# A graph layer on one core: 80 chunks gathered and 63 groups counted, with fp32 one-hots

## The reference

```python
h  = x @ node_w.T
rf = edge_attr_64 @ review_w.T
m  = (h[src] + rf) * edge_weight1
agg = segment_sum(m, dst, num_segments=12500)      # dst is sorted
y = x + agg
out = (y - mean(y)) / sqrt(var(y) + 1e-5)          # over the 64 features
```

## Time and profile before

| what | us |
|---|---|
| median of 3 runs | 4986.41 (4982.99 to 4995.05) |
| the profiled execution: its span, first to last instruction | 4978.1 |
| the profiled execution's own time outside the span | not given; the median lies 8.3 above the span |
| PE busy with matmuls | 2706.6 (54%) |
| DVE busy | 1848.4 (37%) |
| ACT busy | 832.4 (17%) |
| POOL busy | 2097.5 (42%) |
| mean granted TensorE clock | 0.722 of full |

### The profile page before, as it was taken

The page is one execution under the profiler, slowest core; times in us unless marked ns, Lnnn a source line. Parts: engine busy times, 40 slices in busy tenths (PEclk is TensorE's granted clock), DMA queues, the critical chain, the costliest instruction groups (busy, mean ns, idle before and its releaser), DMA issues.

```text
span 4978.1 us, 63532 instructions
## 1 busy us (share of the span) xinstructions
PE 2706.6 (54%) x22003; PEld 2036.4 (41%) x22004; DVE 1848.4 (37%) x7016; ACT 832.4 (17%) x1327; POOL 2097.5 (42%) x2223
## 2 busy tenths in 40 slices
PE   0555555545655545555456555555554556455465
PEld 0343444434443434444344434344443444344345
DVE  3333333423442333333334424333333344333344
ACT  0111111111121111121111211111111112111112
POOL 7343343443334443444433344434444333544432
PEclk9776777767776767777667767677776777667677
DMA  4111121111111111211111211112111112112111
GB/s 98 37 34 37 34 42 38 34 36 38 37 38 38 34 35 38 41 38 34 35 38 35 42 37 35 34 38 42 38 34 35 37 36 42 37 34 43 36 35 38
DMA packets 531458, 192.11 MB, mean 39 GB/s; under 512 B 489893, under 2 KB 495772, under 8 KB 530975
## 3 DMA queue, kind: packets, MB, share of 16 engines
q1 hardware_dynamic: 334128, 80.80, 8.6%
q0 software_dynamic: 70400, 72.23, 6.6%
q10 hardware_dynamic: 126623, 34.94, 3.2%
HBM read 184.60 MB, written 3.20 MB: 38 GB/s over the span
## 4 chain that ended last, share of the span: by engine, by line
PE 43%; another core or an unknown queue 28%; issue 21%; DVE 4%; ACT 2%; DVEq 1%; ACTq 1%; POOLq 0%; POOL 0%
PE x_sums_ps L896 15%; PE count_ps L881 15%; PE window_ps L839 11%; ACT counts L744 2%; DVE scatter L441 1%; DVE hot_lo L497 1%; PE attr_ps L873 1%; ACTq L771 0%; PE turn_ps L858 0%; PE turn_ps L855 0%; DVEq L422 0%; DVEq L425 0%; DVE hot_key L495 0%; PE count_ps L924 0%
## 5 line engine op out<-in xcount | busy, mean ns | idle before, releaser
L366 POOL DMA_INDIRECT rows<-x,src x2200 | 2088.8, 949 | 2791.5 <-DMA src<-src 2146.3
L881 PE MATMUL count_ps<-hot_key,hot_lo 128*128 128x343 bf16 x5550 | 1157.4, 361 | 1294.2 <-ACT counts L744 839.0
L896 PE MATMUL x_sums_ps<-counts,x_tab 128*64 128x126 f32 (+1 forms) x10192 | 865.5, 302 | 790.2 <-issue 775.0
L881 PEld LDWEIGHTS count_ps<-hot_key,hot_lo 128*128 128x128 bf16 x5550 | 570.1, 113 | 1726.5 <-issue 1092.5
L896 PEld LDWEIGHTS x_sums_ps<-counts,x_tab 128*64 128x64 f32 x10192 | 692.5, 154 | 948.4 <-issue 927.3
L744 ACT ACTIVATE counts<-count_ps 128x686 f32<-128x686 f32 x925 | 737.3, 802 | 1784.9 <-remote 1335.6
L495 DVE TENSOR_SCALAR hot_key<-count,cols 128x686 bf16<-128x686 f16 x925 | 377.8, 408 | 1550.8 <-remote 1272.3
L441 DVE TENSOR_SCALAR scatter<-column,dst_left,w 128x128 f32<-128x128 f32 x2200 | 588.3, 347 | 576.2 <-PE window_ps L839 503.0
L497 DVE TENSOR_SCALAR hot_lo<-count,cols 128x128 bf16<-128x128 f16 x2775 | 721.7, 323 | 4.9 <-issue 4.9
L839 PE MATMUL window_ps<-scatter,rows 128*128 128x128 f32 x4400 | 563.1, 289 | 85.2 <-issue 55.4
L839 PEld LDWEIGHTS window_ps<-scatter,rows 128*128 128x128 f32 x4400 | 535.0, 200 | 120.9 <-issue 108.8
(11 more groups left out here) (112 smaller groups left out, 557.5 us busy)
## 6 DMA issues: line engine op xcount, KB each, us to landing
rows<-edge_attr SPq DMA_DIRECT2D x88, 800.0 KB
rows<-x,src POOLq DMA_INDIRECT x2200
g_attr<-edge_attr ACTq DMA_DIRECT2D x51, 576.0 KB
out<-x_tab SPq DMA_DIRECT2D x11, 256.0 KB
counts<-dst SPq DMA_DIRECT2D x1, 1562.5 KB
src<-src SPq DMA_DIRECT2D x88, 12.5 KB, 1.7
dst<-dst SPq DMA_DIRECT2D x88, 12.5 KB
w<-edge_weight SPq DMA_DIRECT2D x88, 12.5 KB
```

Source lines behind the costliest of these rows:

```text
L366: pool.indirect_dma_start(out=rows[:, s, k, 0:F], out_offset=None, in_=x, in_offset=bass.IndirectOffsetOnAxis(ap=src_sb[s][:, k:k + 1].bit ...
L881: last = pe.matmul(count_ps[b][:, a, 0:HALF], hot_lo[h][:, i, :], hot_key[h][:, a * HALF:(a + 1) * HALF], start=(i == 0), stop=(i == 2))
L896: done = pe.matmul(x_sums_ps[half * F:(half + 1) * F, 0:ns], x_tab[:, hi, :], counts[:, hi, 0:ns], start=(hi < 2), stop=(hi >= HI - 2))
```

## The change

Eight chunks less are gathered, and their 200 tiles are counted: 63 groups (0 to 62), the first with 9 tiles. The round becomes ten steps, two of them with two chunks, in a loop of 6 passes, and two last steps of two chunks follow. `hot_key` and `hot_lo` become fp32, `hot_lo` is made once with the whole weight, and the product is two fp32 matmuls. `prepare` and `turn_cols` lose the two cut parts of the weight. `w_both` moves into the space of `counts`, and a store of a block with no whole row of nodes is left out.

```diff
-CHUNKS = 88
-STEPS = (2, 1, 2, 1, 2)
-LAST_STEPS = (2, 2, 2, 2, 2, 2)
+CHUNKS = 80
+STEPS = (1, 1, 1, 1, 2, 1, 1, 1, 1, 2)
+LAST_STEPS = (2, 2)
...
-        KEY, LO, W1, W2, REL, W0 = range(6)
+        KEY, LO, REL, W0 = range(4)
...
-        hot_key = [sb(f"hot_key{b}", [P, HI * SPAN], BF16) for b in range(HOT_BUFS)]
-        hot_lo = [sb(f"hot_lo{b}", [P, 3, P], BF16) for b in range(HOT_BUFS)]
+        hot_key = [sb(f"hot_key{b}", [P, HI * SPAN]) for b in range(HOT_BUFS)]
+        hot_lo = [sb(f"hot_lo{b}", [P, P]) for b in range(HOT_BUFS)]
...
-                    for i, part in enumerate((W0, W1, W2)):
-                        made = dve.tensor_scalar(hot_lo[h][:, i, :], count16[:, 0:P], cols[:, LO, t:t + 1],
-                                                 cols[:, part, t:t + 1], ALU.is_equal, ALU.mult)
+                    made = dve.tensor_scalar(hot_lo[h][:, :], column[:, :], cols[:, LO, t:t + 1],
+                                             cols[:, W0, t:t + 1], ALU.is_equal, ALU.mult)
...
-                    for i in range(3):
-                        for a in range(2):
-                            last = pe.matmul(count_ps[b][:, a, 0:HALF], hot_lo[h][:, i, :],
-                                             hot_key[h][:, a * HALF:(a + 1) * HALF], start=(i == 0), stop=(i == 2))
+                    for a in range(2):
+                        last = pe.matmul(count_ps[b][:, a, 0:HALF], hot_lo[h][:, :],
+                                         hot_key[h][:, a * HALF:(a + 1) * HALF], start=True, stop=True)
```

More of the change, by code:

```diff
@@ L123, in build @@
         g_attr = sb("g_attr", [P, GT, F])
-        hi_lo = sb("hi_lo", [GT, 2, P], I32)
+        src_hi = sb("src_hi", [GT, P], I32)
         tile_first = sb("tile_first", [GT, 1])
-        w_cut = sb("w_cut", [GT, 2, P], BF16)
-        KEY, LO, W1, W2, REL, W0 = range(6)
+        KEY, LO, REL, W0 = range(4)
         packed = sb("packed", [GT, W0, P])
@@ L176, in build @@
         at, g_worst = part(at, 1, [1, 2])
+        at, w_both = part(at, F, [1, 2 * F])
         at, calm = part(at, 1, [4, LATE_CHUNKS])
         assert at <= HI * NS
-        w_both = sb("w_both", [F, 2 * F])
         w_t = sb("w_t", [2 * F, 2 * F])
@@ L334, in _ @@
                     "(a t e) -> a t e", a=1, e=P)).then_inc(g_dst_loaded, 16)
-            sp.dma_start(w_both[:, 0:F], node_w).then_inc(w_loaded, 16)
-            sp.dma_start(w_both[:, F:2 * F], review_w).then_inc(w_loaded, 16)
+            sp.dma_start(w_both[:, 0, 0:F], node_w).then_inc(w_loaded, 16)
+            sp.dma_start(w_both[:, 0, F:2 * F], review_w).then_inc(w_loaded, 16)
             for s in range(SLOTS):
@@ L350, in _ @@
                 whole = min(j, BY_P - h0)
-                sp.dma_start(out[h0 * P:(h0 + whole) * P, :].rearrange("(h l) f -> l h f", l=P),
-                             x_tab[:, h0:h0 + whole, :]).then_inc(stored, 16)
+                if whole:
+                    sp.dma_start(out[h0 * P:(h0 + whole) * P, :].rearrange("(h l) f -> l h f", l=P),
+                                 x_tab[:, h0:h0 + whole, :]).then_inc(stored, 16)
                 if whole < j:
                     sp.dma_start(out[BY_P * P:NODES, :], x_tab[0:NODES - BY_P * P, BY_P, :]).then_inc(stored, 16)
-            sp.wait_ge(stored, 16 * (BLOCKS + (BY_P < HI)))
+            sp.wait_ge(stored, 16 * (sum(h0 < BY_P for h0, _ in blocks) + (BY_P < HI)))
         @block.gpsimd
@@ L466, in prepare @@
                     dve.wait_ge(turned, g)
-                src_i, dst_i, w_i = g_idx[0:nt, 0, :], g_idx[0:nt, 1, :], g_w[0:nt, :]
-                cut, pack, parts = w_cut[0:nt, :, :], packed[0:nt, :, :], hi_lo[0:nt, :, :]
+                src_i, dst_i = g_idx[0:nt, 0, :], g_idx[0:nt, 1, :]
+                pack, hi_i = packed[0:nt, :, :], src_hi[0:nt, :]
                 dve.tensor_reduce(tile_first[0:nt, :], dst_i, AX_X, ALU.min).then_inc(prep_step, 1)
[L470 to L480, removed]
+                dve.tensor_scalar(hi_i, src_i, LO_BITS, None, ALU.arith_shift_right).then_inc(prep_step, 1)
+                dve.wait_ge(prep_step, 4 * g + 2)
+                dve.tensor_scalar(src_i, src_i, P - 1, None, ALU.bitwise_and).then_inc(prep_step, 1)
+                dve.tensor_scalar(pack[:, REL, :], dst_i, tile_first[0:nt, 0:1], None, ALU.subtract
+                                  ).then_inc(prep_step, 1)
+                dve.wait_ge(prep_step, 4 * g + 4)
+                dve.scalar_tensor_tensor(pack[:, KEY, :], hi_i, float(SPAN), pack[:, REL, :],
                                          ALU.mult, ALU.add)
[L482 to L485, removed]
+                dve.tensor_copy(pack[:, LO, :], src_i).then_inc(prepared, 1)
             def make_hot(g, tiles):
@@ L938, in _ @@
             pe.wait_ge(w_loaded, 32)
-            pe.transpose(w_t_ps[:, 0:F], w_both[:, :], ident[0:F, 0:F]).then_inc(w_turned, 1)
+            pe.transpose(w_t_ps[:, 0:F], w_both[:, 0, :], ident[0:F, 0:F]).then_inc(w_turned, 1)
             pe.wait_ge(w_t_ready, 1)
```

## The result

Forecast: 5076 us, slower by 1.8%. Measured: 4831.19 us, median of 4 runs (4823.56 to 4864.78), against 4989.44 (4982.99 to 4995.05) for the kernel before in the same set. The ratio on record, made from all runs, is 0.9699 [0.9665, 0.9733] (the two medians alone give 0.968): faster by 3.0%, outside the range of 4990 to 5225 on the low side. One later kernel, e3_more_records, has a run (4759.51) more than 1.5% above its fastest (4636.36): its ratio leaves that run out, and its trace is of that run. The profiled execution has a span of 4822.8 us, against 4978.1.

What follows compares the result with a forecast made beforehand. Bound: some 60 TensorE instructions pass during a chunk's gathers, about half the span; the rest is TensorE's own speed. 4993 - 24 + 99 = 5068 in the span, 5076 us as median, slower by 1.8%; range 4990 to 5225.

Steps and rivals of the forecast that it cites:

- Bound: Whole kernel: while POOL's gathers fly TensorE passes some 60 instructions, about half the span; the rest is TensorE's own speed.
- Split alone: Fewer gathered chunks and more groups, without fp32: span 4993 us, 15 above 4978.1.
- fp32 at full speed: TensorE's fp32 counting outside the stall: 1.25 us a tile, where bf16 took 0.98 to 1.0.
- rival 3: TensorE counting: fp32 streams one column a cycle, -3.6 us a phase, 4754 us; chance 0.04.
- fp32 counting during a gather: TensorE beside POOL's gathers: 58 instructions at 10 a tile pass 5.8 tiles instead of 4; bounds 4 and 7.3.
- S: Stretch from a gather's start with TensorE counting and `sum_x` in a one-chunk step: mean 67.2 us before, forecast 68.3.
- C: Stretch from a gather's start with TensorE counting in a two-chunk step: mean 54.3 us before, forecast 55.9.
- Phase: A counting phase with split and fp32: 11.6 us left after the stall, 1.6 longer; 62 phases give +99 us.
- Rival 2: Counting during gathers: the stall lets 7.3 of the shorter tiles through, -0.3 us a phase, 4958 us; chance 0.12.
- Rival 1: Counting during gathers: fp32 instructions cost more, only 4 tiles pass, +3.9 us a phase, 5219 us; chance 0.20.
- Rival 4: DVE's longer `hot_key` holds POOL's gathers up, 2 us in each of 62 stretches: +124, 5200 us; chance 0.04.
- -0.5 in S: Shorter DVE one-hots ahead of `scatter` and two transposes less: -0.5 us in each of 48 S, -24 us.

Runs made afterwards that it cites:

- e3_more_records: Kernel after plus one unused one-column fp32 product ahead of each tile's two, with the stall: 4688.53 us, 0.9482 of the kernel before.
- e1: fp32 one-hots alone, without the split (old 88 chunks, 52 groups), against the kernel before, with the stall: 4789.01 us, ratio 0.9736.
- e2: Split alone (80 chunks, 63 groups) with the old three bf16 parts, against the kernel before, with the stall: 4935.32 us, ratio 1.0016.
- i1: Kernel after with eleven one-element POOL fills behind each gather, with the stall: 4028.47 us, 0.8084 of the kernel before.
- j1: Split alone, three bf16 parts, with eleven POOL fills behind each gather, with the stall: 4037.38 us, 0.8068 of the kernel before.
- j2: Split with only two bf16 parts made and multiplied, eleven POOL fills behind each gather, with the stall: 3911.37 us, 0.7831 of the kernel before.
- e5: Split in bf16, TensorE leaving out the third part's products (DVE still makes all three), with the stall: 4659.78 us, 0.9447 of the kernel before.
- f1_after_again: Kernel after, unchanged, run again in a set without the stall: 2903.02 us, 1.0311 of the kernel before.

## Why the prediction was wrong

- **Bound.** Right for this set of runs: for about half of the span TensorE gets through some 60 instructions in 29 us while gathers run. The sentence that this takes 7 us "at full speed" read TensorE's busy time in the stall (7.32 at a clock of 0.56); four tiles at the prediction's own 0.98 are 4 us. Nothing in the sum hangs on it. That the stall isn't in the kernel alone, and that the same program takes 2814 us in another set, no view of one trace could show.
- **Split alone**, +15: right (1.0016). The 2 us in it for group 0 count ten instructions a tile, which is fp32's number and not the split's; that is too small to matter.
- **fp32 at full speed**, 1.25 a tile: right (1.27), and at half clock 4 x 0.57. That rules out rival 3.
- **fp32 counting during a gather**: the step that failed. "58 to 64 instructions, whatever their type and size" gave 58 / 10 = 5.8 tiles. Measured are 97 instructions, 9.7 tiles, in the stretch that stands for 42 of 60, and 70 instructions, 7.0 tiles, in the one that stands for the other 18; 80 or more was the prediction's own sign of being wrong. Two things were wrong. First, I took the beginning of my window for the beginning of the stall: bf16 counting had passed 58 instructions in the first 4 us, fp32 counting needs 8 us for as many, so they lay inside the window. In the 18 that is the only difference from the forecast that the trace shows, and S takes 67.1 where the forecast had 68.3. Second, I took the stall as given whatever the gathers' spacing. In the 42 the first gathers are wider apart, the stall begins 5 us later, and S takes 2.9 us less than in the 18, C 3.4 less. Over the loop that second part is 32 x 2.9 + 10 x 3.4 = 127 of the 235 us; the first is some 48 x 1.2 + 12 x 2.0 = 82.
- **Phase**, +1.6: the one shown lasts from 1996.5 to 2040.5, 44.0 against 46.5. Over both traces a phase of 18 tiles, first matmul to last, has a mean of 45.5 after and 47.5 before, so -2.0. The difference of 3.6 from the forecast, 62 times, is 223 of the error of 245.
- **Rival 2** had the direction and the deciding point (from 7 tiles on). But I bounded it at 58 / 8 = 7.3, so it gave 4958. The bound was taken from the same window, and so a wrong law limited its own rival. It is about right for the 18 stretches (7.0 tiles): had all been like them, the span would be some 127 longer, about 4950, and rival 2 had 4969 - 19 = 4950 for the span.
- **Rival 1** (fp32 dearer in the stall): not seen. **Rival 4**: its premise is seen, its price isn't. `hot_key` takes 585 ns in place of 408, inside the bounds, POOL's gathers a mean of 969 in place of 949, and 126 of 2000 last over 1.1 us where 11 of 2200 did. At 20 ns more for each of 2000 gathers that is 40 us of POOL in all, not 124; and 40 of the 126 are a chunk's first, where the stretches are the shorter ones.
- **-0.5 in S**: can't be told apart from the rest of S.

What is shown: fp32 makes the gain (e1, e2), it is made in the counting beside gathers, and idle fills between the gathers remove most of the stall (i1, j1, j2). That the wider first gathers make 42 stretches shorter is read from one trace, in which they come first; no run set those gathers apart alone. Other traces agree in part: in e5 the 54 stretches with a spacing over 1.35 among the first two pass a median of 84 instructions, the other 6 pass 60, but in e2, with three bf16 parts, 9 such stretches pass 73 and the other 51 pass 74. Nor is it shown why they are wider in 42 stretches and not in 18. What is described but not explained is the number of instructions that pass: counted over 32 us from the gather's start, a median of 112 before (100 to 128), 117 after (97 to 132), 117 in e5 (91 to 127).

What stays open is what holds TensorE's instructions back, why 1.25 us and 1.5 us or more differ so much, and why some sets have no stall. The wide spacing alone isn't what keeps TensorE going: in f1_after_again a chunk's gathers are on average 1.25 to 1.29 us apart too, and it never stalls. Three runs that would tell more weren't made where the stall is: six fills in place of eleven, POOL idle between gathers without any instruction (the fills and the spacing were always changed together), and 15 of 25 gathers. Two causes are made less likely, slower transfers of the gathered rows and late loads of instructions. The DMA queues of the page, the kernel after in its first run:

```profile
q0 software_dynamic: 64000, 65.66, 7.1%
...
q8 instruction: 204, 3.34, 0.3%
```

f1_after_again, the same program without the stall:

```profile
q0 software_dynamic: 64000, 65.66, 11.8%
...
q8 instruction: 204, 3.34, 0.5%
```

The columns are packets, MB and share of 16 engines' span. 7.1% of 4822.8 and 11.8% of 2900.8 are both 342 us, so the gathers' packets take as long with the stall as without. The instruction loads are as many and, within the rounding, as long. Their times in the trace of the kernel after don't follow the pauses either: in the stretches whose first pause is at 8.4 us a load of q8 comes 4.7, 5.7, 8.4 or 11.2 us after the first gather's start, in those with 13.8 at 4.5, 8.1, 9.3 or 12.0.

## What to carry to other kernels

A law read from a window holds for that window and its pace of issue: count from the event that starts the effect, in small bins, before a slower or faster instruction stream is put in its place. Where an engine pauses for no reason that the trace names, first run the kernel in more than one set of runs and move the suspected neighbour (here its spacing, by idle fills); that was worth 19% (1.0016 in e2, 0.8068 in j1), six times the change. One stretch is a sample, too: sort all stretches of a trace before one of them is taken for the rule. And an edit tuned against such a pause can be a loss elsewhere: this one is 0.970 with the stall and 1.031 without it. Of the full computations the best are the split alone (0.944) where there is no stall, and the split with pauses (0.807) or fp32 with pauses (0.808) where there is.

## What was not expected of the hardware

- One program, two paces: 4928 to 4997 us in four sets of runs (with that of the result), and 2812 to 2816 in three. By chip, by host or by time isn't shown.
- Idle fills of 0.4 to 0.6 us on POOL behind each gather take 803 us off, with the stall; the same costs 355 us without it (3258.0 against 2903.0).
- A product of one column in fp32, with its weight load, costs 0.26 us a tile at full clock.
- Gathers last 0.94 us beside a quiet DVE and 1.17 to 1.29 in e3's free stretch, where DVE is busy 11.4 us of 29. The Trainium skill, SBUF — State Buffer, section "Who interferes with whom", says that DVE in a two-port mode and GpSimd lock each other out. Whether these one-hots run in such a mode no run here shows. The trace of e3 agrees in the direction, with 0.2 to 0.35 us a gather at most; but in f1_after_again gathers last 0.94 to 1.01 us beside a DVE busy 16.1 us of 29, so a busy DVE by itself doesn't make them long.
